# A two-layer block on one core: row maxima of the first unit of heads moved from behind the delta net's loop into its last three steps

## The reference, cut to what matters

```python
# delta net, per batch and head (16 heads of 8), over 1024 time steps
M = M * b_t[:, :, None, None] + (k_t[:, :, None] * v_t[:, None, :])[:, None]
Z = Z * b_t[:, :, None] + k_t[:, None, :]
num, den = einsum('bd,bcde->be', q_t, M), einsum('bd,bcd->b', q_t, Z) + EPS
y_t = num / den[:, None]                       # then @ Wo + bo, residual, layer norm

# attention: 4 batches, 16 heads of 8, 4 key heads, 1024 tokens, causal
attn = einsum('bqhd,bkhd->bhqk', q, k) * scale
attn = softmax(where(causal, attn, -inf), axis=-1)
out = einsum('bhqk,bkhd->bqhd', attn, v)
```

## Time and profile before

| what | value |
|---|---|
| median of three runs | 1553.66 us |
| the profiled execution | 1556.09 us |
| its span | 1554.8 us |
| PE, busy | 1189.6 us (77%) |
| DVE, busy | 1145.6 us (74%) |
| ACT, busy | 734.7 us (47%) |
| POOL, busy | 707.1 us (45%) |
| granted TensorE clock over the span | 0.875 of full |

### The profile page before, as it was taken

The page is one execution under the profiler, slowest core; times in us unless marked ns, Lnnn a source line. Parts: engine busy times, 40 slices in busy tenths (PEclk is TensorE's granted clock), DMA queues, the critical chain, the costliest instruction groups (busy, mean ns, idle before and its releaser), DMA issues.

```text
span 1554.8 us, 18685 instructions
## 1 busy us (share of the span) xinstructions
PE 1189.6 (77%) x5568; PEld 543.2 (35%) x5568; DVE 1145.6 (74%) x3003; ACT 734.7 (47%) x1599; POOL 707.1 (45%) x857
## 2 busy tenths in 40 slices
PE   3415987998888886566848677898989898988873
PEld 1112454555444433223312222333333333333222
DVE  5888646757977987869859787787888788877022
ACT  4644783364332354123230266656565656555741
POOL 7334672556775686446660122123413341334244
PEclk9856998999998988776865698999999999989996
DMA  3000104221110100003125101101021202000010
GB/s 106 0 0 1 46 1 127 83 65 55 39 41 30 33 22 0 0 1 66 35 49 82 24 1 26 35 16 36 4 33 16 35 5 32 4 1 3 1 41 14
DMA packets 33666, 47.02 MB, mean 30 GB/s; under 512 B 5007, under 2 KB 18191, under 8 KB 33263
## 3 DMA queue, kind: packets, MB, share of 16 engines
q1 hardware_dynamic: 30974, 43.84, 12.7%
q10 hardware_dynamic: 2592, 2.00, 0.5%
HBM read 39.14 MB, written 6.68 MB: 29 GB/s over the span
## 4 chain that ended last, share of the span: by engine, by line
PE 30%; DVE 21%; ACT 6%; POOL 4%; issue 4%; DMA 0%; ACTq 0%; DVEq 0%; POOLq 0%
PE PS L653 8%; PE PS L611 5%; PE PS L636 5%; DVE PS L1168 4%; DVE SS L1171 3%; PE PS L698 3%; DVE RB L1085 3%; PE PS L310 2%; ACT RB L1574 2%; PE PS L497 2%; DVE st L740 1%; ACT RB L1581 1%; DVE PS L1065 1%; DVE B L1085 1%; PE PS L678 1%
## 5 line engine op out<-in xcount | busy, mean ns | idle before, releaser
L1574 ACT ACTIVATE RB<-PS 128x512 f32<-128x512 f32 (+3 forms) x768 | 328.2, 497 | 268.9 <-PE PS L636 265.1
L611 PE MATMUL PS<-B 96*128 96x512 bf16 (+3 forms) x768 | 259.7, 361 | 54.8 <-DVE B L1214 23.6
L1823 POOL TENSOR_SCALAR_AFFINE_SELECT RB<-RB 128x512 f32<-128x512 f32 x128 | 81.2, 634 | 414.1 <-ACT RB L1574 414.1
L1168 DVE CUSTOM_DVE_ANT_0 PS<-PS,w_msk 128x128 f32<-128x128 f32 (+3 forms) x512 | 244.2, 506 | 29.3 <-PE PS L611 28.8
L636 PE MATMUL PS<-B 96*128 96x512 bf16 (+3 forms) x768 | 242.8, 339 | 18.5 <-ACT RB L1574 16.9
L1171 DVE TENSOR_REDUCE SS<-PS 128x1 f32<-128x512 f32 x256 | 176.0, 687 | 38.5 <-PE PS L611 37.6
L653 PE MATMUL PS<-RB,B 128*32 128x512 f32 (+3 forms) x1536 | 171.9, 520 | 14.4 <-ACT RB L1581 14.4
L611 PEld LDWEIGHTS PS<-B 96*128 96x128 bf16 x768 | 77.2, 102 | 205.1 <-DVE SS L1168 63.2
L1742 POOL TENSOR_TENSOR RB<-RB,B 128x512 f32<-128x512 f32 x64 | 84.8, 1328 | 98.4 <-DVE RB L978 77.2
L636 PEld LDWEIGHTS PS<-B 96*128 96x128 bf16 x768 | 75.6, 100 | 100.1 <-ACT RB L1574 59.3
L497 PE MATMUL PS<-B,WW 128*128 128x512 f32 x128 | 84.9, 800 | 32.8 <-DVE RB L1085 22.7
(11 more groups left out here) (243 smaller groups left out, 2259.0 us busy)
## 6 DMA issues: line engine op xcount, KB each, us to landing
B<-scrW SPq DMA_DIRECT2D x128, 128.0 KB, 3.0
B<-scrQ SPq DMA_DIRECT2D x72, 128.0 KB
scrQ<-B SPq DMA_DIRECT2D x6, 384.0 KB, 6.4
B<-scrK SPq DMA_DIRECT2D x36, 64.0 KB
X<-in_x SPq DMA_DIRECT2D x8, 256.0 KB, 8.6
out_dram<-X SPq DMA_DIRECT2D x8, 256.0 KB, 3.0
B<-in_w SPq DMA_DIRECT2D x3, 576.0 KB, 4.8
B<-in_zeros SPq DMA_DIRECT2D x9, 128.0 KB
```

Of the source, the lines that this page charges most:

```text
L611: pe.matmul(p[:, 0:w], qs[u % 3][:, h, 128 * i:128 * i + 128], keys_of(u, h)[:, 512 * c:512 * c + w], start=True, stop=True).then_inc(s["m ...
L1168: ins = dve.tensor_tensor_reduce(p, p, msk[:, 512 - w:512], 1.0, LOWEST, ALU.add, ALU.max, MX[:, u % 2, i, h, c:c + 1])
L1574: act.activation(RB[:, 4 * (step % 3) + z, 0:w], bank(bank_of["score", step, z])[:, 0:w], ACT.Exp).then_inc(s["ex2"], 1)
L1823: pool.affine_select(out=pb, in_=pb, compare_op=ALU.is_ge, fill=0.0, base=0, pattern=[[0, 4], [1, 128]], channel_multiplier=-1).then_inc(s ...
```

## The change

The 96 maxima of unit 0 are issued in the delta net's steps 36, 37 and 38, 32 in each. In each of these steps they stand ahead of everything else on PE (the query sums, the passage's slices) and on DVE (the passage's slices). They use banks 4, 5, 0 and 1 in place of the ring of banks 3 to 6. `ready_1(0)` stands at the head of step 36 on PE. `first_1` now takes the bank as an argument. The programs of ACT, POOL and SP are not changed.

```diff
+        FIRST_AT = 36
+        FIRST_BANKS = (4, 5, 0, 1)
+
+        def first_unit(step):
+            return range(32 * (step - FIRST_AT), 32 * (step - FIRST_AT) + 32) if step >= FIRST_AT else []
...
             value_c(0)
             for step in range(C_STEPS):
+                if step == FIRST_AT:
+                    ready_1(0)
+                for n in first_unit(step):
+                    first_1(FIRST_BANKS[n % 4], 0, n)
                 if 0 <= step - 2 < 36:
                     query_c(step - 2)
...
-            ready_1(0)
-            for n in range(96):
-                first_1(0, 0, n)
             guard_1(0)
...
-                        first_1(step, v, n)
+                        first_1(next_1(step), v, n)
...
             for step in range(C_STEPS):
                 units = [v for v in beside(step) if v < 9 * NG]
+                for n in first_unit(step):
+                    highest(0, n)
                 if step < 36:
                     value_c(step)
...
-            for n in range(96):
-                highest(0, n)
             guard(0)
             guard_row(0)
```

More of the change, by code:

```diff
@@ L584, in pass_f, with first_1, ready_1 @@
                     bank_of["pj_e", b, 3] = i
+            def first_1(k, u, n):
+                h, i, c = FIRST[n]
+                p = room(k)
+                w = first_width(i, c)
+                pe.matmul(p[:, 0:w], qs[u % 3][:, h, 128 * i:128 * i + 128],
+                          keys_of(u, h)[:, 512 * c:512 * c + w], start=True, stop=True).then_inc(s["mm1"], 1)
+                banks.lend(k, s["mx1"], 96 * u + n + 1)
+                bank_of["first", u, n] = k
+            def ready_1(u):
+                pe.wait_ge(s_q[u % 3], 192 + 160 * (u // 3))
+                pe.wait_ge(s_k[u // 2 % 2], 192 + 144 * (u // 4))
             value_c(0)
             for step in range(C_STEPS):
+                if step == FIRST_AT:
+                    ready_1(0)
+                for n in first_unit(step):
+                    first_1(FIRST_BANKS[n % 4], 0, n)
                 if 0 <= step - 2 < 36:
@@ L604, in next_1 @@
                 return 3 + ring_1[0] % 4
[L606 to L618, removed]
             def guard_1(u):
@@ L1141, in part_e, with highest @@
                 dve.tensor_tensor(o[:, 2, :], p, o[:, 1, :], ALU.subtract).then_inc(last, 1)
+            def highest(u, n):
+                h, i, c = FIRST[n]
+                dve.wait_ge(s["mm1"], 96 * u + n + 1)
+                w = first_width(i, c)
+                p = bank(bank_of["first", u, n])[:, 0:w]
+                if c == i // 4:
+                    ins = dve.tensor_tensor_reduce(p, p, msk[:, 512 - w:512], 1.0, LOWEST, ALU.add, ALU.max,
+                                                   MX[:, u % 2, i, h, c:c + 1])
+                else:
+                    ins = dve.tensor_reduce(MX[:, u % 2, i, h, c:c + 1], p, AX, ALU.max)
+                ins.then_inc(s["mx1"], 1)
             for step in range(C_STEPS):
                 units = [v for v in beside(step) if v < 9 * NG]
+                for n in first_unit(step):
+                    highest(0, n)
                 if step < 36:
@@ L1159, in vector_program @@
                     pass_f(b, k)
[L1162 to L1172, removed]
             def guard(u):
```

## The result

The changed kernel takes 1581.68 us (median of 4 runs, 1580.66 to 1583.72 us); the kernel before took 1554.1 us beside it (4 runs). The ratio on record is 1.0164 with a 95% interval of 1.0137 to 1.0191; the quotient of these two medians is 1.0177, inside it. The profiled execution has a span of 1582.4 us, 27.6 us more than before. The forecast was 1580.8 us.

What follows compares the result with a forecast made beforehand. No one engine bounds the kernel; the stretch is a hand-over between two loops, with maxima and loads as nearly equal branches. Step 0 27.2 us later on the 1553.66 us median gives 1580.8 us, range 1574 to 1589 us.

Steps and rivals of the forecast that it cites:

- last cut of batch 2: DVE's last piece of the batch 2 passage, written out by SP: forecast at 860.2 us, 41.7 us later.
- guard rows ready: Unit 0's rows, made after its maxima for SP to write and read back: forecast at 863.8 us, 5.5 us earlier.
- loads begin: SP starts loading batch 1's keys and unit 2's queries once the cut is home: 862.9 us, 30.1 us later.
- loads drained: The key and query loads finish moving: the same 33.7 us as before, so at 896.6 us.
- step 0: First matmul of the last phase, waiting for the guard's read: forecast at 901.3 us, 27.2 us later.
- The deciding step: At the guard's write on SP: its bytes stand behind the late loads, so step 0 comes 27.2 us later.
- the shift stays to the end: In the last phase nothing can use the pause, so the 27.2 us delay remains in the total.
- DVE's pause ahead of the second third: Between the first two runs of 32 maxima: DVE idle from 812.4 to 817.1 us behind PE's queries and transposes.
- one steady share: Bound on the key and query loads' drain: their DMA share was taken as steady, giving +-1.5 us.
- Rival 1: Guard's transfers wait only for the loads' issue, not their bytes: +3.3 us, 1557 us; chance 0.06.
- Rival 2: SP's order does not bind, loads issued before guard rows are made: 5.5 us earlier, 1548.2 us; chance 0.03.
- Rival 3: Larger bubbles between the thirds of the maxima, 5 us more at each: +37 us, 1591 us; chance 0.06.

Runs made afterwards that it cites:

- e1: Changed kernel with the guard's write and read back moved ahead of the key and query loads in SP's order; 1550.60 us, seam 71.1 us.
- e3: Changed kernel with the loads of batch 1's keys and unit 2's queries issued by ACT instead of SP; 1554.74 us, ratio 0.999.
- e4: Changed kernel with only the first 32 maxima in step 36, the other 64 behind the loop, SP's order kept; seam 77.2 us.
- e6: Changed kernel with only the key load left ahead of the guard, the query load behind it; 1559.39 us, ratio 1.0012.
- e7: Changed kernel with only 32 maxima in step 36 and the guard ahead of the loads on SP; seam 68.7 us.
- e8: Changed kernel with 110 more unused matmuls keeping PE busy before step 0; 1579.22 us, ratio 1.0135.
- e5: e7 with query matmuls ahead of the maxima on PE and 40 maxima spread over three steps, 56 behind the loop; 1548.26 us, ratio 0.9934.

## Why the prediction was right

It gave 1580.8 us, the four runs 1581.68 us, well inside 1574 to 1589 us. Its own steps, in us behind the last scan:

| step | forecast | measured |
|---|---|---|
| DVE ends the first third | 15.5 | 15.3 |
| DVE begins the second third | 20.2 | 18.0 |
| DVE begins the last third | 45.1 | 43.0 |
| last cut of batch 2 | 63.3 | 61.7 |
| guard rows ready | 66.9 | 65.1 |
| loads begin | 66.0 | 64.3 |
| loads drained | 99.7 | 101.1 |
| guard's write seen by SP | 101.2 | 102.5 |
| step 0 | 104.4 | 106.3 |

**The deciding step held.** Of the two branches that leave the last cut, the prediction took the transfers for the longer one, and e1 shows it by its removal: seam 106.3 to 71.1 us. That the shift stays to the end held too: 680.7 against 681.7 us.

**Two sizes were off, in opposite directions.** DVE's pause ahead of the second third was 2.7 us, not 4.7; the one ahead of the last third, with slices 11 and 12 in it, came out as forecast, 9.2 us. In the first of them the query matmuls took 3.05 us in place of 3.78 and the transposes 1.04 us in place of 1.97, because the granted clock rose while this float32 work ran (0.86 of full in the window of 810 to 812 us); I had priced them at the lower level of 1.2 GHz on which the maxima run. With a first third that was 0.2 us shorter this makes up most of the 2.2 us by the start of the second third. In return the drain took 36.8 us and not 33.7, outside the 1.5 us either way that the bounds allowed. The prediction based that bound on "one steady share", which the windows of the kernel before do not show: between 834 and 864 us the share of single windows of 2 us goes from 0.25 to 0.79 and the rate from 31 to 123 GB/s. The read with its first matmul took 3.8 in place of 3.2 us. Together with the cut that came 1.6 us early this is +2 us on the seam, which the 2.5 us of a shorter first stretch hid by luck: the total is nearer to the forecast than its terms are.

**Rival 1** (only the issue counts) gave step 0 at 80.5 us behind the scan and is refuted by the 28.5 us of the write. Nor would a queue of its own have made it right: in e3 the read, alone in SP's queue, had no packet under way until the loads handed over before it were through. **Rival 2** (faster) failed where the prediction said, at SP's order; e1, which takes just this away, reaches 71.1 us, where the rival stood at 868.6 - 796.9 = 71.7 us. **Rival 3** (larger pauses) did not come; the pauses were smaller.

## What to carry to other kernels

When work is moved ahead of other work on an engine, list what the delayed work releases, and above all which transfers: here a gain of 7 us was real, and a delay of 40 us of one 384 KB write turned it into +28 us, through a queue whose program the change never touches. A transfer that the next phase waits for should not stand behind large ones that are needed later; in the changed kernel moving that one line took 35.2 us off the seam, while moving the 96 matmuls is worth 7. And two branches of nearly equal length that leave one event must be shortened together: shortening one alone gives at most their difference, 2.9 us here, and gave nothing in e4, whose loads took 2.6 us longer to drain. Delaying the common event costs almost in full: of the 40.0 us of the last cut, 28.4 us reached the loads, since the cut was home after 2.6 us instead of 14.2.

## What the runs showed of the hardware

A small transfer waits for the bytes that were handed over before it and are still to be moved: the guard's write of 48 KB took 1.5 us with nothing ahead (before, e1), 8.6 us in e6, 10.8 us in e4 and 28.5 us in the changed kernel, and landed 1.3 to 1.5 us after the drain of what stood ahead in the last three. Another queue did not free it: in e3 the read of 48 KB, issued by SP at 867.23 us, had its first packets between 874 and 875 us, behind 768 KB that ACT had handed over, with eight of sixteen engines' worth of DMA time free.

The same 24 loads drained in 26.6 us (e7), 27.9 us (e1), 33.7 us (before), 36.3 us (e4) and 36.8 us (after). The mean share of the DMA engines in these stretches was 0.50, 0.49, 0.52, 0.52 and 0.52, so each packet took longer. It was not PE's activity or clock (e8). The last phase running beside them does not explain it alone: e6's query load moved at 60 to 73 GB/s beside it and e5's at 75, e1's at 101. But e5 and e6 ran on another chip than e1, e4 and e7, and no run takes the chip out of the comparison. The cause stays open.

PE's granted clock was 0.50 (1.2 GHz) in every window of the maxima in the kernel before, for example from 834 to 838 us, in which PE ran score matmuls for 3.44 of 4.00 us. In the changed kernel it rose to 0.86 and 0.74 in the windows 810 to 812 and 830 to 832 us, each time while PE ran the float32 matmuls between the thirds one after another.
